# The output product of four small heads: one step of sixteen matmuls in place of three steps

## The reference

```
x = x + attn_norm(layernorm(x))      # 16 heads of 8 channels, all keys, q and k normalised per head
x = x + local_stack(layernorm(x))    # 6 layers of windowed attention (16 heads of 64) and a gated MLP
x = x + attn_latent(layernorm(x))    # 16 heads of 8 channels, causal, q/k/v through 32 latent channels
x = x + local_stack(layernorm(x))
x = x + attn_linear(layernorm(x))    # linear attention
x = x + swiglu(layernorm(x))
x = x + attn_plain(layernorm(x))     # 16 heads of 8 channels, causal
x = x + swiglu(layernorm(x))
```

```
scores = q @ k.T / sqrt(8)                  # 512 x 512; latent and plain: causal mask
att    = softmax(scores)
out    = att @ v                            # 512 x 8
x      = x + concat(out of 16 heads) @ w_o
```

## Time and profile before

| | |
|---|---|
| median of 3 runs | 4350.73 us (4345.05 to 4351.43) |
| the profiled execution | 4349.36 us, its span 4347.4 us |
| TensorE busy | 4061.2 us, 93% |
| VectorE busy | 3351.6 us, 77% |
| ScalarE busy | 2915.0 us, 67% |
| GpSimd busy | 2390.7 us, 55% |
| output product (L1329) | 1536 instructions, 127.3 to 4319.3 us |
| granted TensorE clock, mean | 0.97 of full speed |

### The profile page before, as it was taken

One profiled execution on the slowest core, in us unless ns is written; L12 is line 12 of the kernel. 1 busy time (PEld: TensorE's weight loads), 2 busy tenths in 40 slices (PEclk: granted clock), 3 DMA queues, 4 the chain that ended last, 5 costly groups with the idle time before them and its releaser, 6 DMA issues. The chain is left out here.

```text
span 4347.4 us, 128585 instructions
## 1 busy us (share of the span) xinstructions
PE 4061.2 (93%) x53847; PEld 2019.5 (46%) x53847; DVE 3351.6 (77%) x5020; ACT 2915.0 (67%) x7325; POOL 2390.7 (55%) x1684
## 2 busy tenths in 40 slices
PE   5998999999999999998979999999999999987897
PEld 3223555545555554553435555455554555543443
DVE  3776888888888888885658888888888888865664
ACT  2765777777777777774557777777777777755554
POOL 3314766666666666664227666667666666641120
PEclk7999999999999999998999999999999999999998
DMA  4121000000000000001220000000000000000110
GB/s 166 57 60 31 2 22 7 2 21 7 22 7 2 22 7 2 2 2 57 64 65 2 2 21 7 21 7 4 24 2 21 7 2 2 2 10 18 50 58 8
DMA packets 68917, 97.79 MB, mean 22 GB/s; under 512 B 34472, under 2 KB 58756, under 8 KB 62340
## 3 DMA queue, kind: packets, MB, share of 16 engines
q1 hardware_dynamic: 67476, 83.28, 6.4%
q10 hardware_dynamic: 864, 6.29, 0.4%
HBM read 72.18 MB, written 16.78 MB: 20 GB/s over the span
## 5 line engine op out<-in xcount | busy, mean ns | idle before, releaser
L402 POOL TENSOR_TENSOR ra<-ra,rb 128x1024 f32<-128x1024 f32 x384 | 927.7, 2416 | 328.7 <-DVE rb L741 328.6
L416 POOL TENSOR_TENSOR qkr<-ra,inv 128x1024 f32<-128x1024 f32 x384 | 731.3, 1904 | 612.7 <-ACT inv L680 609.0
L448 PE MATMUL ps<-wvo,xs 128*32 128x512 f32 x6144 | 820.9, 606 | 72.3 <-ACT vs L602 72.3
L493 PE MATMUL ps<-wq,xs 128*128 128x512 f32 x1536 | 749.7, 611 | 7.2 <-DVE rb L741 4.5
L653 ACT ACTIVATE pr<-ps,neg 128x64 f32<-128x64 f32 x3072 | 670.3, 338 | 7.1 <-DVE neg L718 7.1
L602 ACT ACTIVATE vs<-ps 128x512 f32<-128x512 f32 x768 | 451.2, 588 | 226.7 <-PE ps L448 225.7
L515 PEld LDWEIGHTS ps<-kt,qt 64*32 64x32 f32 x24576 | 359.6, 107 | 293.2 <-issue 290.3
L718 DVE TENSOR_REDUCE neg<-ps 128x8 f32<-128x512 f32 x384 | 263.7, 687 | 279.2 <-PE ps L515 272.7
L493 PEld LDWEIGHTS ps<-wq,xs 128*128 128x128 f32 x1536 | 275.6, 192 | 434.7 <-issue 335.9
L738 DVE TENSOR_TENSOR ra<-ps,rope 128x1024 f32<-128x1024 f32 x384 | 451.8, 1177 | 23.4 <-ACT sq L627 16.2
L1505 DVE TENSOR_REDUCE nm<-ps 128x1 f32<-128x512 f32 (+3 forms) x768 | 378.3, 549 | 117.6 <-PE ps L1270 115.2
(11 more groups left out here) (251 smaller groups left out, 6203.4 us busy)
## 6 DMA issues: line engine op xcount, KB each, us to landing
wq<-in_L_ffn_Wqkv SPq DMA_DIRECT2D x12, 1024.0 KB, 5.2
wvo<-wvo_scratch SPq DMA_DIRECT2D x12, 1024.0 KB, 4.8
wvo_scratch<-pt ACTq DMA_DIRECT2D x6, 1024.0 KB, 4.1
w<-in_L_ffn_W SPq DMA_DIRECT2D x12, 341.0 KB
qs<-norm_pieces SPq DMA_DIRECT2D x9, 384.0 KB
ks<-norm_pieces SPq DMA_DIRECT2D x9, 384.0 KB
qs<-latent_pieces SPq DMA_DIRECT2D x9, 384.0 KB
ks<-latent_pieces SPq DMA_DIRECT2D x9, 384.0 KB
```

The costliest lines, as they stand in the source:

```text
L402: pool.tensor_tensor(ra[:, m % 2, :, :], ra[:, m % 2, :, :], rb[:, :, :], ALU.add).then_inc(sum_done.sem, 1)
L416: pool.tensor_tensor(qkr[:, m % 2, :, :].rearrange("p s (h c) -> p (s h) c", c=HD), ra[:, m % 2, :, :].rearrange("p s (h c) -> p (s h) c", ...
L448: last = pe.matmul(VP[32 * j:32 * j + 32, :], xs[:, turn % 2, v * WIN:v * WIN + WIN], wvo[l % 2][:, j, :], start=True, stop=True)
L493: last = pe.matmul(PJ[:, qk, :], xs[:, turn % 2, t * P:t * P + P], wq[l % 2][:, at:at + 512], start=True, stop=True)
```

## The change

The table `AV_AT` gets one entry in place of three: all four blocks of keys are multiplied where k mod 4 = 1, in the order block by block and head by head as before. The semaphore waits ahead of the first matmul and the increment of `av_mm` behind the last follow the smallest and the largest entry of the table, which are now the same. Nothing else moves.

```diff
-    AV_AT = {1: (0,), 2: (1,), 3: (2, 3)}
+    AV_AT = {2: (0, 1, 2, 3)}
...
             for at, blocks in AV_AT.items():
                 if (g := group_at(k, 4 + at)) is not None:
-                    if at == 1:
+                    if at == min(AV_AT):
                         if kind == "plain" and g == 0:
                             source.x_final(pe, BATCH - 1)
                         pe.wait_ge(exp_done.sem, exp_done.at(4 * NP * (g + 1)))
...
-                    if at == 3:
+                    if at == max(AV_AT):
                         last.then_inc(av_mm.sem, 1)
```

## The result

The changed kernel took 4369.21 us (median of 7 runs, 4355.23 to 4371.83), the kernel before 4345.05 beside it on the same chip (7 runs, 4340.54 to 4351.43): ratio 1.0048 [1.0034, 1.0062]. The change costs 0.48%, about 21 us by that ratio (the two medians lie 24 apart). The likeliest case of the forecast, a difference within 0.2%, did not come; the sign of its sum (+4) did, at a fifth of the size. The time lies 2 us above the range's end.

What follows compares the result with a forecast made beforehand. No engine was taken as full in norm, TensorE as nearly the bound in causal; +10 norm, -7.5 causal and +1 DMA gave +4 on 4349.36, 4353, or 4355 as median (1.4 above); range 4344 to 4367.

Steps and rivals of the forecast that it cites:

- The likeliest case of the forecast: Whole kernel: norm and causal stages cancel, 4347 to 4362 us, within 0.2% of the kernel before; chance 0.6.
- the sign of its sum (+4): Whole kernel: slower, as norm +10, causal -7.5 and the maxima's DMAs +1 were summed to +4 us.
- Step 1: Output product on TensorE: merging bursts saves 0.28 us a group in norm, 0.30 in causal; 14 us if TensorE alone paced.
- The rival built on that alone: Whole kernel: TensorE bounds everywhere and only burst overhead counts, -14 us, 4337; norm cycles below 12.8; chance 0.1.
- Step 2: Norm stage: without bursts between items VectorE paces, regular cycles 13.82 us for 12.88, taken as +1.0 each; +10 in all.
- the ScalarE bound of 13.1: Norm cycle if VectorE does not decide: ScalarE's exponentials, copy `ou` and the burst sum to 13.1 us, +0.2.
- The -0.5 for the drain: Norm stage's drain, where few scores are left: a gain of about 0.5 us.
- Step 3: Causal stages: VectorE never holds TensorE; 14 regular cycles gain 0.15 us, 18 others 0.3; -7.5, bounds 0 and -10.
- the delay of T2 by `ou`: Causal cycles: `ou` between the exponentials of items 2 and 3 delays a turned-score piece of item 3 by some 0.25 us.
- the full -0.3: Causal cycles with layer norm, output projection or SwiGLU, about 18 of 32: each keeps the whole burst saving of 0.3 us.
- Step 4: Maxima's transpose and DMAs, needed by item 3: 0.3 us less time between, rare wait grows; +1 us, bound +10.
- The second rival: Whole kernel: norm's cushion loss is larger, +14 us, and causal stages give nothing back: 4365 to 4375; chance 0.3.

Runs made afterwards that it cites:

- burst_item0: The changed kernel with the merged burst of all four blocks one item earlier, in item 0, in all stages: 4349.09 us, 1.0003 to the kernel before.
- norm_late: The changed kernel with VectorE's transpose, reciprocal and product after a group one item later, under the merged burst, in all stages: 4359.39 us, 1.003 to the kernel before.
- causal_merged: The kernel before with the one-step table in the two causal stages (latent and plain) alone, three steps kept in norm: 4351.7 us, 1.0008 to the kernel before.
- ou_early: The changed kernel with ScalarE's copy `ou` one item earlier, directly behind the merged burst: 4372.91 us, 1.0065 to the kernel before.
- norm_merged: The kernel before with the one-step table in the norm stage alone, three steps kept in the causal stages: 4362.99 us, 1.0037 to the kernel before.
- late_vector: The kernel before, three bursts kept, with two unused transposes of `ou` added ahead of VectorE's work after a group in norm: 4366.14 us, 1.0044 to it.

## Why the prediction was partly right

- **Step 1, the burst overhead: right.** 3.57 and 2.30 us were measured for the 3.57 and 2.28 forecast. The Trainium skill, TensorEngine Tiling (Array Packing), section Key Properties, says that a change of tiling mode drains TensorE; the trace agrees in direction, with 0.28 us less for two bursts fewer a group, 0.14 each. The rival built on that alone (TensorE the bound everywhere, 4337) fell: norm cycles came at 13.78, not under 12.8.
- **Step 2, the lost cushion in norm: mechanism and regular size right.** 13.82 forecast, 13.78 measured, the wait at S3 and VectorE's 2.80 us of idle time as described; burst_item0 and norm_late removed it. That they landed on 13.05 and 13.06 for the ScalarE bound of 13.1 does not show that bound: in burst_item0 a second VectorE chain, over the transpose of the maxima, gives the same time, and the sums had left it out. Over twelve cycles it cost 7.8, where the step had +10.8: the layer-norm cycles came at +0.5, 0 and -0.1 instead of +0.6 each, and two further cycles, 13.8 long before already, gained nothing and lost nothing. The -0.5 for the drain is not seen: what stands behind the twelve cycles is 1.1 us longer (59.71 for 58.62, at a clock of about 0.8 in both kernels), what stands ahead of them 1.1 shorter, and the twelve cycles hold the norm stage's 14.8.
- **Step 3, causal: failed.** "I take half of the 0.30 for the regular cycles: -0.15" measured -0.04 at best (0.01 or 0.02 more against other regular cycles of the kernel before), and "-7.5" for the stages measured +2.6 in the profiled execution and +3.5 by causal_merged's median. I had named the delay of T2 by `ou`; ou_early showed that moving `ou` changes nothing in that cycle, while in the plain stage's cycles with other work it does. What goes with the lost saving is a late T0 at an item boundary without a burst; there are three in a cycle where there was one, and the four items take 0.24 us longer. The cushion argument of step 2 would explain it, for ScalarE and two banks of turned scores, and I had applied it to VectorE alone; no experiment took this wait away. The rest of the difference lies in the cycles with other work, which did not keep "the full -0.3", and in a lower clock (latent 0.91 after, 0.95 before).
- **Step 4, the maxima by DMA: about right.** 2.6 us became 3.2 in four cases; +1 had been taken.
- **The missing term: the granted clock.** The forecast held TensorE's pace fixed and priced waits alone. A lower clock took about 7 us of norm's 14.8 in the profiled execution. Over the timed runs the core's mean granted clock was 0.966 after and 0.972 before (medians of 7 and of 73). In norm_late's runs 0.008 more went with some 12 us less, and so it did in the runs of the kernel before (0.968 to 0.976, 4353.5 to 4341.2 on average): 1.5 for each 0.001. By that 9 of the 21 us, an estimate. The second rival (4365 to 4375) named the time that came and one of its causes, the causal stages giving nothing back; its other cause, a larger cushion loss, was not it.

In one account, by ratios: norm +16 (forecast +10), causal +3.5 (forecast -6.5); together 19.5 of the 21 measured. About 8 of norm's 16 are the cushion. That the other 8 are the clock is read from one profiled execution; the runs bear it out only in part, since norm_merged's mean clock was 0.970 for 0.972, which by the same 1.5 is 3 us.

**What stays open.** Why the clock falls is not settled. Waits of 1.31, 1.59 and 1.72 us on S3 stand right before it in three kernels, and waits of 0.94 in late_vector's regular cycles do not bring it. But no length of wait parts the cases. In the changed kernel's timeline a burst behind 1.28 us ran at full clock and one behind 0.78 did not:

```profile
181.04 0.39 PE L1270 MATMUL ps<-ks,qs 72*128 72x512 bf16 x1 [1.28 <-DVE nm L1505]
...
181.57 3.64 PE L1329 MATMUL ps<-pt,va 128*32 128x512 f32 x32
...
274.60 0.39 PE L1270 MATMUL ps<-ks,qs 72*128 72x512 bf16 x1 [0.78 <-DVE nm L1505]
...
275.30 5.11 PE L1329 MATMUL ps<-pt,va 128*32 128x512 f32 x32
```

In ou_early a wait of 1.75 (166.98) was followed by a burst of 3.57. Nor does the sum of TensorE's listed waits from 130 to 310 us part them: 9.3 us in the kernel before (clock 1.00), 15.5 in the change (0.94), but 8.3 in burst_item0 and 8.1 in norm_late (0.95 both). In norm_late half clock follows 2.5 us behind a wait of 1.26 in a layer-norm cycle, and the kernel before has waits of that size in the same place and kept 1.00. So that the change's waits cause its lower clock is not shown; what is shown is that every kernel with merged norm bursts was granted less there. The clock also differs between kernels with the same norm stage: 0.94, 0.88 and 0.86 in the change, norm_merged and ou_early. The 1.8 us in the first local stack, whose code is untouched, go with a lower clock at its two ends, as given above; why it was lower was not tried. And burst_item0 and norm_late have 10 us between their medians, of which the causal stages are a part, with a clock of 0.969 and 0.9645 over their runs; why norm_late is granted less was not tried. Nor is the clock a tight measure of the time: of the changed kernel's runs at 0.967 one took 4355.23 and one 4370.19.

## What to carry to other kernels

Between two engines that pass work through a few banks, a burst of other work on the first is the second's time to catch up: merging bursts saves a fixed 0.15 us each here and takes one catching-up away each, so count the banks and price both before merging, for every consumer and not only the busiest. Two equal bursts were still a gain (12.79 us a norm cycle for 12.88), one was not (13.78). Where a long burst must be, place it over the consumer's own extra work: one item earlier, the same merged burst cost 0.03% instead of 0.48%. When a cycle comes out where a bound had put it, take a term of that bound away before believing it: without `ou`, 13.04 stayed 13.04. And compare TensorE's granted clock before and after in every stage: here the waits were not the whole price.

## What the runs showed of the hardware that was not expected

- TensorE went to half clock in stages in which it was busy for nine tenths of the time (162.20 of 180 us from 130 to 310 us, clock 0.94), and stayed there for stretches of some 4 to 14 us (up to 17 in norm_merged). The Trainium skill, TensorE: Matmul & The Clock Gate, section What's actually happening, gives the two levels, 1.2 and 2.4 GHz; the trace agrees, with matmuls of 0.38 and 0.63 us.
- At half clock a step of eight f32 matmuls took 1.86 us for 1.00 (late_vector, 257.60 to 259.46, clock 0.50), and an S or T product went from 0.22 to 0.43 between starts. The bursts of 32 took up to 6.27 us for 3.57, and not twice as long, because the clock came back before their end: in norm_merged's burst of 6.25 us it was 0.50 for 5 us and 0.82 in the last 1.25.
- Adding useless products to fill TensorE's gaps did not keep the clock up (0.96 and 0.95 with, 0.94 without) and cost 0.65% and 1.24% against the kernel before.
